# Windowed attention on one core: the position bias moves from TensorE to VectorE, the subtraction of the maximum to GpSimd, the exponential one slot later, the reciprocal root into four parts

## What is computed

```python
shortcut = x
h = layernorm(x, norm1_g, norm1_b)                 # then cut into 1024 windows of 64 tokens
qkv = hw @ qkv_w + qkv_b
attn = jnp.einsum('bhnd,bhmd->bhnm', q * SCALE, k)
attn = jax.nn.softmax(attn + bias[None], axis=-1)  # bias[h, n, m]: the same for every window
out = jnp.einsum('bhnm,bhmd->bhnd', attn, v)
x = shortcut + (out @ proj_w + proj_b)
x + gelu(layernorm(x, norm2_g, norm2_b) @ fc1_w + fc1_b) @ fc2_w + fc2_b
```

## Time and profile before

| | us |
|---|---|
| median of 3 runs (lowest, highest) | 1194.38 (1191.48, 1198.63) |
| the profiled execution, its own time | 1193.66 |
| its span, first to last instruction | 1191.9 |
| mean granted TensorE clock | 0.994 |
| busy: TensorE / VectorE / ScalarE / GpSimd | 1128.3 / 874.4 / 892.2 / 514.9 |

### The profile page before, as it was taken

The page is one execution under the profiler, slowest core; times in us unless marked ns, Lnnn a source line. Parts: engine busy times, 40 slices in busy tenths (PEclk is TensorE's granted clock), DMA queues, the critical chain, the costliest instruction groups (busy, mean ns, idle before and its releaser), DMA issues.

```text
span 1191.9 us, 28977 instructions
## 1 busy us (share of the span) xinstructions
PE 1128.3 (95%) x7876; PEld 1004.1 (84%) x7876; DVE 874.4 (73%) x2757; ACT 892.2 (75%) x2755; POOL 514.9 (43%) x790
## 2 busy tenths in 40 slices
PE   2999999999999999999999999999989999999997
PEld 2888888888888888888888888888879999999997
DVE  4777777777777777777777777777767777777773
ACT  2877888888778888887788888877866676676674
POOL 3233322222333222223332222233358888888882
PEclk9999999999999999999999999999989999999999
DMA  1000100000001000000010000000001111111111
GB/s 48 18 27 30 36 31 32 30 26 26 26 30 37 30 33 30 26 26 26 30 36 31 32 29 26 26 26 31 24 1 40 40 42 45 45 40 40 40 40 53
DMA packets 24744, 38.26 MB, mean 32 GB/s; under 512 B 4055, under 2 KB 20634, under 8 KB 24730
## 3 DMA queue, kind: packets, MB, share of 16 engines
q1 hardware_dynamic: 24730, 38.10, 10.2%
HBM read 25.50 MB, written 12.58 MB: 32 GB/s over the span
## 4 chain that ended last, share of the span: by engine, by line
PE 70%; ACT 22%; issue 5%; DVE 1%; POOL 1%; DMA 0%; SPq 0%; ACTq 0%; POOLq 0%
PE scores_ps L527 14%; PE mixed_ps L480 7%; PE scores_ps L463 7%; ACT k_blocks L691 7%; PE kv_ps L447 5%; ACT v_blocks L702 5%; PE kv_ps L454 5%; PE q_ps L453 5%; PE probs_t_ps L470 4%; PE scores_ps L459 4%; ACT tokens_t L679 3%; PE turn_ps L491 3%; ACT probs L707 3%; PE kv_ps L520 3%; PE heads_t_ps L491 2%
## 5 line engine op out<-in xcount | busy, mean ns | idle before, releaser
L350 POOL TENSOR_TENSOR small<-stats 128x16 f32<-128x16 f32 x64 | 14.9, 233 | 612.5 <-DVE stats L810 612.5
L691 ACT ACTIVATE k_blocks<-kv_ps 32x128 f32<-32x128 f32 x768 | 204.6, 266 | 87.8 <-PE kv_ps L454 81.8
L480 PEld LDWEIGHTS mixed_ps<-v_blocks,probs_t 128*128 128x128 f32 x1536 | 191.5, 191 | 30.5 <-issue 13.5
L480 PE MATMUL mixed_ps<-v_blocks,probs_t 128*128 128x66 f32 x1536 | 209.4, 272 | 4.2 <-ACT probs_t L684 1.7
L463 PE MATMUL scores_ps<-k_blocks,q_blocks 96*128 96x192 f32 x1024 | 209.7, 327 | 0.0
L365 POOL TENSOR_TENSOR rstd<-small,minus_half 128x16 f32<-128x16 f32 x64 | 208.2, 3253 | 0.0
L916 DVE TENSOR_REDUCE row_top<-scores_ps 128x6 f32<-128x384 f32 x256 | 142.7, 557 | 78.0 <-PE scores_ps L463 74.5
L527 PEld LDWEIGHTS scores_ps<-wfc,hidden 128*128 128x128 f32 x1536 | 181.5, 192 | 5.3
L527 PE MATMUL scores_ps<-wfc,hidden 128*128 128x96 f32 x1536 | 180.1, 274 | 0.0
L463 PEld LDWEIGHTS scores_ps<-k_blocks,q_blocks 96*128 96x128 f32 x1024 | 178.0, 190 | 0.0
L920 DVE TENSOR_TENSOR lowered<-scores_ps,row_top 128x384 f32<-128x384 f32 x256 | 142.7, 557 | 44.6 <-ACT probs L707 32.7
(11 more groups left out here) (109 smaller groups left out, 1994.7 us busy)
## 6 DMA issues: line engine op xcount, KB each, us to landing
x_in<-in_x SPq DMA_DIRECT2D x256, 48.0 KB
x<-in_x SPq DMA_DIRECT2D x128, 96.0 KB
out<-x SPq DMA_DIRECT2D x128, 96.0 KB
pos_in<-in_L_conv_rel_bias_table SPq DMA_DIRECT2D x8, 10.6 KB
wfc_in<-in_L_conv_fc_w SPq DMA_DIRECT2D x2, 36.0 KB
wqkv_in<-in_L_conv_qkv_w SPq DMA_DIRECT2D x2, 27.0 KB
wfc<-in_L_conv_fc_w SPq DMA_DIRECT2D x2, 24.0 KB
gains<-in_L_conv_norm_g SPq DMA_DIRECT2D x2, 0.2 KB
```

What stands on the lines that cost most here:

```text
L480: mm = pe.matmul(mixed_ps[:, MIX * h:MIX * h + MIX], probs_t[:, h, :], v_blocks[:, k % V_BUFS, h, :], start=True, stop=True)
L691: ins = act.activation(k_blocks[rows, k % 2, :, h, :], kv_ps[rows, at:at + 2 * TOK].rearrange("p (a t) -> p a t", a=2), ACT.Copy)
```

## The change

- The bias is no longer a matmul. Once, in the set-up, TensorE spreads it over 128 partitions and VectorE keeps it as `pos` (128 x 192, f32).
- VectorE `top(g, k)`: `biased` = scores + `pos`, from PSUM to SBUF (two buffers), then the row maximum from `biased`. It waits for `lowered_ok` of g-2 in place of `probs_ok` of g-1.
- GpSimd `lower(g, k)`: `lowered` = `biased` - maximum, in SBUF (two buffers).
- ScalarE does `exp` of slot k in slot k+1, right behind `probs_t_out` and ahead of `k_out`.
- `scores(k)` waits for `biased_ok` of slot k-2.
- GpSimd's layer norm of the front is now written between the eight `lower`: the sums behind slot 1's, centring in two halves and a quarter of the root behind slot 2's, and so on. The front's root is four instructions of 128 x 4.
- VectorE's second part of the statistics (11 groups) stands at the end of slot 0 in place of slot 1 (but for the first batch).
- `norm_back(0)` is written between the `lower` of the last batch; `norm_back(1)` comes behind the last of them.

```diff
+            def front_sums(n):
+                pool.wait_ge(stats_ok, n + 1)
+                norm_sums(pool, FRONT_STEPS * n, small_step)
+            def front_centre(n):
+                for w in range(2):
+                    centre(pool, x_groups, slice(WIN * w, WIN * w + WIN), small_step)
+                pool.wait_ge(small_step, FRONT_STEPS * n + 8)
+            def front_root(half, w):
+                at = WIN * w + HALF * half
+                root(pool, slice(at, at + HALF), small_step)
+            def front_scale(n, half):
+                pool.wait_ge(small_step, FRONT_STEPS * n + 12 + 2 * half)
+                wait(pool, turned, 2 * n - 1 + half)
+                scale_half(pool, half, normed[:, :, :].rearrange("p j (w c) -> p w j c", w=2)).then_inc(normed_ok, 1)
...
+            def lower(g, k):
+                wait(pool, max_ok, g + 1)
+                wait(pool, probs_ok, g - 1)
+                pool.tensor_tensor(lowered[:, k % 2, :, :], biased[:, k % 2, :, :],
+                                   broadcast(row_top[:, k % 2, :], 2, TOK), ALU.subtract).then_inc(lowered_ok, 1)
...
+            def body(n, first, last):
+                for k in range(QUADS):
+                    lower(QUADS * n + k, k)
+                    if not last:
+                        if k == 1:
+                            front_sums(n + 1)
+                        if k == 2:
+                            front_centre(n + 1)
+                            front_root(0, 0)
+                        if k == 3:
+                            front_root(0, 1)
+                            front_scale(n + 1, 0)
+                        if k == 4:
+                            front_root(1, 0)
+                            front_root(1, 1)
+                        if k == 5:
+                            front_scale(n + 1, 1)
...
             def scores(k):
                 bank = scores_ps[k % 2]
 
-                pe.matmul(bank[:, 0:2 * HEADS * TOK], flip_r[:, :], pos[:, :, :].rearrange("p a n -> p (a n)"),
-                          start=True, stop=False, skip_group_check=True)
...
-                    wait(pe, lowered_ok, g0 + k - 1)
+                    wait(pe, biased_ok, g0 + k - 1)
...
+            def exp_of(g, k):
+                wait(act, lowered_ok, g + 1)
+                exp(k)
...
                         wait(act, probs_turned, g0 + k - 1)
                         probs_t_out()
+                    if not (first and k == 0):
+                        exp_of(g0 + k - 1, (k - 1) % QUADS)
                     if k % 2 == 0 and not (first and k == 0):
 
                         k_out(k + 1)
...
-
-                    wait(act, lowered_ok, g0 + k + 1)
-                    exp(k)
...
-            def lower(g, k):
-
-                rows = scores_ps[k % 2][:, 0:2 * HEADS * TOK].rearrange("p (r t) -> p r t", t=TOK)
-                dve.tensor_reduce(row_top[:, k % 2, :], rows, AX.X, ALU.max).then_inc(max_ok, 1)
-                dve.wait_ge(max_ok, g + 1)
-
-                wait(dve, probs_ok, g)
-                dve.tensor_tensor(lowered[:, :, :, :].rearrange("p a h t -> p (a h) t"), rows,
-                                  broadcast(row_top[:, k % 2, :], 2, TOK), ALU.subtract).then_inc(lowered_ok, 1)
+            def top(g, k):
+                rows = scores_ps[k % 2][:, 0:2 * HEADS * TOK]
+                wait(dve, lowered_ok, g - 1)
+                dve.tensor_tensor(biased[:, k % 2, :, :].rearrange("p (a h) t -> p a (h t)", a=2),
+                                  rows.rearrange("p (a n) -> p a n", a=2), broadcast(pos[:, :], 1, 2), ALU.add
+                                  ).then_inc(biased_ok, 1)
+                dve.wait_ge(biased_ok, g + 1)
+                dve.tensor_reduce(row_top[:, k % 2, :], biased[:, k % 2, :, :], AX.X, ALU.max).then_inc(max_ok, 1)
...
-                    if k == 1 and not last:
+                    if k == (1 if first else 0) and not last:
                         stats_front(n + 1, 1)
```

More of the change, by code:

```diff
@@ L194, in swin_block @@
         scores_mm = sem("scores_mm")
+        biased_ok = sem("biased_ok")
         max_ok = sem("max_ok")
@@ L423, in norm_back @@
[L423 to L431, removed]
+            x_groups = x_in[:, :].rearrange("p (g c) -> p g c", c=C)
+            def front_sums(n):
+                pool.wait_ge(stats_ok, n + 1)
+                norm_sums(pool, FRONT_STEPS * n, small_step)
@@ new lines, in back_scale @@
+            def back_scale(n, half):
+                wait(pool, turned2, 2 * n - 1 + half)
+                target = normed2[:, :, :, 0:C].rearrange("p j w c -> p w j c")
+                scale_half(pool, half, target).then_inc(normed2_ok, 1)
+            def lower(g, k):
[3 more added lines that the diff above has]
+                                   broadcast(row_top[:, k % 2, :], 2, TOK), ALU.subtract).then_inc(lowered_ok, 1)
@@ new lines, in _ @@
+            front_sums(0)
+            front_centre(0)
+            for half in range(2):
+                front_root(half, 0)
+                front_root(half, 1)
+                front_scale(0, half)
+            def body(n, first, last):
[15 more added lines that the diff above has]
+                            front_scale(n + 1, 1)
+                    else:
+                        if k == 1:
+                            back_sums(0)
+                            back_centre(0)
+                        if k == 2:
+                            back_root(0)
+                        if k in (3, 4):
+                            back_scale(0, k - 3)
@@ L432, in _, with norm_back @@
+            batches(pool, body)
+            def norm_back(n):
+                back_sums(n)
+                back_centre(n)
+                back_root(n)
+                for half in range(2):
+                    back_scale(n, half)
             with pool.Fori(1, BATCHES) as n:
@@ L619, in _ @@
             pe.wait_ge(pos_ok, 1)
+            pe.matmul(heads_t_ps[:, 0:HEADS * TOK], flip[:, :, :].rearrange("p b q -> p (b q)"),
+                      pos_all[:, :, :, :].rearrange("p h i j -> p (h i j)"), start=True, stop=True).then_inc(pos_mm, 1)
             batches(pe, body)
@@ L865, in _ @@
                                        [REL, WIN], [1, WIN]])
[L866 to L874, removed]
-                dve.tensor_copy(pos[0:TOK, a, :], pos_high[0:TOK, :].bitcast(F32))
-                ins = dve.tensor_tensor(pos[TOK:2 * TOK, a, :], pos_flat[TOK:2 * TOK, :],
-                                        pos_high[TOK:2 * TOK, :].bitcast(F32), ALU.subtract)
-            ins.then_inc(pos_ok, 1)
+            dve.tensor_copy(pos_all[:, :, :, :], wide).then_inc(pos_ok, 1)
             def other_weights():
@@ L961, in body @@
                     wait(dve, scores_mm, g0 + k + 1)
-                    lower(g0 + k, k)
+                    top(g0 + k, k)
                     if k == 3 and not first:
```

75 lines of the change are left out of this document (39 added, 36 removed).

## The result

| us | before | changed |
|---|---|---|
| median (lowest to highest) of 5 runs each, same chip | 1194.36 (1191.48 to 1198.63) | 1204.6 (1203.92 to 1207.41) |
| the profiled execution, its span | 1193.66, 1191.9 | 1205.63, 1203.9 |
| a batch of the loop | 26.47 | 26.52 |

The account below looks back on a forecast made before the run. It took the front as a loop passing between TensorE and ScalarE. Terms 0.41 + 0.05 + 0.12 - 0.17 = +0.41 a batch, times 30 = +12.3, plus 2.5 once, on 1193.66 gave 1208.5; range 1186 to 1224.

Parts of the forecast that it names:

- The statistics into slot 0: VectorE's 11 groups, 1.31 us, push ahead of slot 1's addition, delaying it to 453.78; slot 1's bias gain is overtaken.
- The chain that it makes, +0.41: Slot 1: `lowered(1)` ready at 455.88, ScalarE there at 455.47, so `k_out(3)` and head projection come 0.41 later; 52%.
- The exponential a slot later, "nothing": Even slots: ScalarE's work up to `k_out` keeps the same sum with the exponential behind `probs_t_out`, so no change.
- +0.05 into slot 5: The heads copy moves ahead of `probs_t_out`, which then waits for the turned probabilities: +0.05 us a batch.
- +0.12: Slot 5: the exponential no longer fills ScalarE's time before the turned tokens come; +0.12 us, bounds 0 and 0.53.
- The bias matmul: Removing it from TensorE gains 0.17 per slot that counts, slots 1 and 5; slot 1's is overtaken, leaving -0.17 a batch.
- GpSimd's subtraction: The 128 x 384 subtraction moved to GpSimd takes 0.83 us, bounds 0.74 and 1.03.
- The quarter root: Each quarter of GpSimd's front root costs 0.87 us, bounds 0.73 and 2.93; no loss while under about 1.2.
- a sign of being wrong: Waits of TensorE for `normed` that `scores(7)` shows were listed as evidence against the prediction.
- Loop: The 30 batches of the loop, each +0.41 us, together +12.3.
- Once only, +2.5: Outside the loop: set-up +1.2, last batch and hand-over to the back +1.3.
- TensorE's clock falls: Rival: about 3 us idle a batch drops TensorE to 1.2 GHz through slots 1 to 3, up to 1440; 2%.

Follow-up runs that it names:

- the warmed kernels: 22 discarded matmuls in TensorE's set-up: on the changed kernel 1201.03, on the kernel before 1194.99; with statistics in slot 1 and first-batch discarded matmuls too, 1181.29.
- filling the first batch: The changed kernel with a discarded 128 x 384 fp32r matmul ahead of each scores in the first batch only: 1202.07, ratio 1.0036.

## Why the prediction was right and wrong

Direction and size of the whole were right, for reasons of which half held.

- **The statistics into slot 0**: right, in mechanism and in total. Forecast 0.41 of delay plus 0.17 of gain overtaken, 0.58; measured 0.55 at the head projection, 8.64 without the move and 9.19 with it. The split between its two parts was not right: 0.25 of delay and 0.30 of gain overtaken, and 0.18 of that gain is the exponential's, which I had at nothing (0.09 each at 0-1 and 2-3).
- **The chain that it makes, +0.41**: mis-sized. Measured +0.25 (8.94 to 9.19). The failed step is the handover: I took 0.55 from an exponential to ScalarE's next start, read where the next one is the heads copy; ahead of `k_out` it is 0.43 (468.51 to 468.94). The other 0.04 is `exp(1)`, at 6.55 in place of 6.59.
- **The exponential a slot later, "nothing"**: failed. It wins 0.25 a batch. "+0.05 into slot 5" was -0.07 (interval 4-5), "+0.12" was +0.03 (interval 6-7).
- **The bias matmul**: 0.12 at each of slots 1 and 5 against 0.17. It pays where TensorE is waited for and nowhere else, as forecast; TensorE's 49 us of busy time (70 were forecast) bought some 7, and in the changed kernel, where slot 1's part is overtaken, some 4.
- **GpSimd's subtraction**: 828 ns against 0.83. The ratio of 1.96 of the Trainium skill ("GPSIMD Engine Reference", 3. Performance versus the Vector engine), by which it would have taken 1.09 us, an estimate, does not hold for this operation.
- **The quarter root**: 1.01 against 0.87, so the fixed part is larger than two sizes of another operation suggest. Under the 1.2 at which I said it would matter. TensorE does wait 0.60 for `normed` before it turns the second half (31 times, 19.7 us, one of them 1.7 in the set-up), and `scores(7)` is late by 0.13 (0.99 behind `k_out(7)`, 0.86 with the root in one instruction). I had called that a sign of being wrong; it costs nothing, since it is taken back before `k_out(0)` (interval 7-0: 4.43).
- **Loop**: 0.05 x 30 = +1.5 (1.2 between the events above), not +12.3.
- **Once only, +2.5**: failed, and this is where the time is. The set-up did cost 1.45 (`scores(0)` at 27.80, now 29.25; forecast 1.2) and the end won 1.4 where I had +1.3, with a clock that differs there too. What I left out is the clock of the first two batches: 12.2 less 1.45, some 11 us. For 7.4 of them it is shown, by the same program's two executions; the rest goes with a half level that lasts longer than before (43 us against 31 to 35), but was not isolated. I had read the clock column alone, which says 1.00 there, and never compared durations at the start with those of the loop.
- **"TensorE's clock falls", 2%**: too little. I had priced it as an event of every batch and argued that the new front was denser than the one stretch I looked at. It came at the start, and the root in one instruction shows it in the loop, with 0.28 us more idle TensorE a batch than the kernel as changed.

That 1204.6 lies near 1208.5 is therefore partly luck: -11 in the loop and +8 once only.

What stays open: why the half level lasts until 31 to 35 us in one kernel and 43 to 52 in the other. The runs show that an early rise doesn't last (the warmed kernels all fell again). Whether filling the first batch stops the second fall isn't shown: the trace with it has none, but neither has the second trace of the changed kernel without an edit. Which waits decide the rises and the falls wasn't isolated.

## What to carry over

Before work is moved off a busy TensorE, ask whether the busy time is what keeps its clock up: look at durations and counts of the same matmul, not at the clock column alone, at the start above all. Work moved ahead of a critical chain on an engine that is "25% idle" costs by how late it makes the chain (here 0.57 of the 1.30 that was moved), whatever the idle share says; split a batch at the pacing engine's repeated instruction, and each change shows up in one interval. A gain per batch must be re-read in the handovers around the new neighbour, since the same exponential hands over in 0.43 or in 0.55 us by what follows it.

## What the runs showed that I had not expected

- A half-clock stretch at the start, until 31 us before and until 52 us in the changed kernel, that the granted-clock column gives as 1.00.
- The same program with its rise at 43 or at 52 us, with or without a second fall, 6.4 us apart. The Trainium skill ("TensorE: Matmul & The Clock Gate", What's actually happening) says that the number of slow matmuls at the start varies from run to run; the trace agrees.
- With waits of 0.62, 0.42 and 0.74 us in slots 5 to 7 of every batch the clock fell in one batch of about seven, where the same kernel with 1.1 us a batch more TensorE work never fell in its loop.
- The root on 4 columns takes 1.01 us, on 16 columns 2.93.
